# The last two attention steps of an audio tower: the softmax product on GpSimd, with sums and reciprocals in SBUF

## What is computed

```python
tokens = einsum('bnpd,edp->bne', patches(x), W) + b      # 16-sample patches, stride 8: 93 tokens
h = tokens
h = h + attn(layernorm(h))     # 8 heads of 64, a 3-tap causal convolution on q, k, v, ALiBi bias
h = h + ffn(layernorm(h))      # top-2 of 16 experts; each expert's hidden units are averaged over its tokens
# inside attn, per sequence and head (93 x 93 scores):
sim  = q @ k.T + bias, masked above the diagonal
attn = softmax(sim)            # exp(sim - max), divided by its row sum
out  = attn @ v
```

## Time and profile before

| | before |
|---|---|
| median of 3 runs | 741.98 us (741.1 to 743.17) |
| the profiled execution | 745.71 us, span 744.0 us, mean granted clock 0.984 |
| TensorE busy | 698.2 us, 94% |
| ScalarE busy | 603.1 us, 81% |
| VectorE busy | 572.5 us, 77% |
| GpSimd busy | 379.3 us, 51% |
| line 1242, product on VectorE | 64 instructions, 8 of them in steps 17 and 18 |

### The profile page before, as it was taken

How to read it: one execution, slowest core, us unless ns; L and a number is a source line. 1 busy time by engine, 2 the same in 40 slices (tenths; PEclk the granted TensorE clock), 3 DMA queues, 4 the chain that set the end, 5 groups by cost and what they waited for, 6 DMA issues and landing times.

```text
span 744.0 us, 21223 instructions
## 1 busy us (share of the span) xinstructions
PE 698.2 (94%) x6576; PEld 625.4 (84%) x6576; DVE 572.5 (77%) x1593; ACT 603.1 (81%) x2014; POOL 379.3 (51%) x392
## 2 busy tenths in 40 slices
PE   6889999999999999999999999998888898999996
PEld 6878888988888988889898989886776687999994
DVE  6166778788788788887787888788898768988876
ACT  4457889999898989899998989787877786899860
POOL 5652335676665665766666666554363557222200
PEclk9899999999999999999999999999999999999997
DMA  8132133341222211212212122102024123222206
GB/s 315 32 85 63 42 100 104 104 125 49 70 54 60 65 52 52 57 49 55 52 52 76 51 57 57 51 12 72 22 75 172 49 58 74 61 66 63 63 19 166
DMA packets 44274, 54.01 MB, mean 73 GB/s; under 512 B 13651, under 2 KB 31251, under 8 KB 43696
## 3 DMA queue, kind: packets, MB, share of 16 engines
q1 hardware_dynamic: 30048, 38.84, 17.9%
q0 software_dynamic: 12544, 12.87, 6.5%
q10 hardware_dynamic: 1616, 1.48, 0.6%
HBM read 42.69 MB, written 10.26 MB: 71 GB/s over the span
## 4 chain that ended last, share of the span: by engine, by line
PE 44%; DVE 28%; ACT 18%; issue 7%; DVEq 1%; DMA 1%; POOL 0%; ACTq 0%
ACT prob L909 11%; PE psTP L506 6%; DVE qkv L1101 5%; DVE qkv L1104 5%; PE psTP L508 5%; PE psTP L507 5%; PE psSO L788 4%; PE psTP L788 4%; DVE prob L1242 4%; PE psTP L580 3%; PE psSO L600 3%; PE psSO L655 3%; DVE rmin L1193 3%; PE psSO L636 3%; ACT qkv L878 3%
## 5 line engine op out<-in xcount | busy, mean ns | idle before, releaser
L1499 POOL DMA_INDIRECT expert_rows<-hn,slot x128 | 168.3, 1315 | 52.3 <-issue 32.0
L909 ACT ACTIVATE prob<-psSO,rmin 93x93 f32<-93x93 f32 x512 | 152.1, 355 | 9.1 <-DVE rmin L1193 8.6
L1417 POOL TENSOR_TENSOR x_lo<-x_raw,x_hi 128x752 fp32r<-128x752 f32 x58 | 105.0, 1811 | 46.4 <-ACT x_hi L870 45.9
L1101 DVE SCALAR_TENSOR_TENSOR qkv<-psTP,taps,qkv 128x368 f32<-128x368 f32 x192 | 112.7, 587 | 20.1 <-ACT qkv L878 18.4
L878 ACT ACTIVATE qkv<-psTP,taps 128x372 f32<-128x372 f32 x192 | 113.2, 590 | 9.2 <-PE psTP L508 8.7
L1104 DVE SCALAR_TENSOR_TENSOR qkv<-psTP,taps,qkv 128x364 f32<-128x364 f32 x192 | 114.5, 596 | 6.8
L909 ACT ACTIVATION_READ_ACCUMULATOR prob<-psSO,rmin 93x1 f32 x512 | 98.3, 192 | 0.0
L506 PE MATMUL psTP<-x_hi,wtok_hi 128*128 128x376 f32 x232 | 88.5, 381 | 1.0 <-POOL x_lo L1417 1.0
L506 PE MATMUL psTP<-xnT_hi,wqkv_hi 128*128 128x372 f32 x192 | 77.4, 403 | 8.3 <-DVE qkv L1104 7.7
L508 PE MATMUL psTP<-x_hi,wtok_lo 128*128 128x376 f32 x232 | 78.0, 336 | 0.0
L507 PE MATMUL psTP<-x_lo,wtok_hi 128*128 128x376 f32 x232 | 77.9, 336 | 0.0
(11 more groups left out here) (212 smaller groups left out, 1746.2 us busy)
## 6 DMA issues: line engine op xcount, KB each, us to landing
x_raw<-in_x SPq DMA_DIRECT2D x58, 376.0 KB
w1s<-in_w POOLq DMA_DIRECT2D x8, 512.0 KB
w<-in_w SPq DMA_DIRECT2D x4, 1024.0 KB
out<-resid SPq DMA_DIRECT2D x16, 160.0 KB, 2.6
xsE<-expert_rows SPq DMA_DIRECT2D x36, 64.0 KB, 2.0
xs<-expert_rows SPq DMA_DIRECT2D x36, 64.0 KB, 1.8
xs<-expert_rows POOLq DMA_DIRECT2D x36, 64.0 KB, 2.1
x_first_raw<-in_x SPq DMA_DIRECT2D x6, 376.0 KB, 6.6
```

The lines of the kernel that those rows point to most:

```text
L909: i = nc.scalar.activation(prob[:, a, hh, :], psS[:NT, a, hh * NT:(hh + 1) * NT], ACT.Exp, bias=rmin[:, a, hh:hh + 1], scale=-1.0, accum_o ...
L1101: nc.vector.scalar_tensor_tensor(dst[:, :, 1:NT], src[:, :, 0:NT - 1], taps[:, k, 1:2], dst[:, :, 1:NT], ALU.mult, ALU.add).then_inc(tap1_ ...
L1417: nc.gpsimd.tensor_tensor(lo[:, 0:PIECE], src, hi[:, 0:PIECE].bitcast(F32), ALU.subtract)\
L1499: nc.gpsimd.indirect_dma_start(rows, bass.IndirectOffsetOnAxis(slot[1 - u][:, c:c + 1], 0), hn[1 - u][:, c % GB, :], None)\
```

## The change

In steps 17 and 18 the sums and their reciprocals lie in two new SBUF tensors, `den_late` and `rden_late`, in place of PSUM, which GpSimd can then read. The reciprocal stays on VectorE. The product leaves VectorE's queue and becomes an instruction on GpSimd's, with the same tensor and a broadcast of the reciprocals. In GpSimd's slot it stands behind the four normalisation instructions (slot 1) and ahead of the slot's scatters. The other steps are as before.

```diff
--- before.py
+++ after.py
@@ -123,6 +123,7 @@
         wtok_raw = early0[:, 0:P * D].rearrange("p (s j e) -> p s j e", s=GB, j=4)
         wqkv_raw = early0[:, P * D:P * D + NBLK * 128].rearrange("p (k c) -> p k c", c=128)
         rmin = sb("rmin", [NT, 2, 4])
+        den_late, rden_late = sb("den_late", [NT, 2, 4]), sb("rden_late", [NT, 2, 4])
         prob = sb("prob", [NT, 2, 4, NT])
         probT = sb("probT", [NT, 2, 4, NT])
         attnT = sb("attnT", [128, QB, NT])
@@ -213,8 +214,7 @@
 
             if not isinstance(t, int) or t <= NG:
                 return psS[:NT, :, 4 * NT:4 * NT + 4], psS[:NT, :, 4 * NT + 4:4 * NT + 8]
-            bank = psTok if t == NG + 1 else psP[0]
-            return tuple(bank[:NT, at:at + 8].rearrange("p (a h) -> p a h", a=2) for at in (496, 504))
+            return den_late[:, :, :], rden_late[:, :, :]
 
         psOut = [psX4[:NT, :, :] for psX4 in psMix]
 
@@ -420,6 +420,10 @@
         def at(t, s, *slots):
 
             return isinstance(t, int) and (t - NG, s) in slots
+
+        def pool_divides(t):
+
+            return isinstance(t, int) and t > NG
 
         def late_slot(t, s):
 
@@ -1238,10 +1242,11 @@
                     if prev and f.proj and not f.tok and not f.norm:
                         residual(n, psWout)
                     if f.attn:
-                        dve.wait_ge(rden_done, n + 1)
-                        nc.vector.tensor_tensor(prob[:, :, :, :], prob[:, :, :, :],
-                                                rden.unsqueeze(3).broadcast_to([NT, 2, 4, NT]),
-                                                ALU.mult).then_inc(prob_ready, 1)
+                        if not pool_divides(t):
+                            dve.wait_ge(rden_done, n + 1)
+                            nc.vector.tensor_tensor(prob[:, :, :, :], prob[:, :, :, :],
+                                                    rden.unsqueeze(3).broadcast_to([NT, 2, 4, NT]),
+                                                    ALU.mult).then_inc(prob_ready, 1)
                     if f.proj and (f.tok or f.norm):
                         conv(t, u, 3 * s + 1)
                     if prev and (f.tok or f.norm or not f.proj) and not at(t, s, (2, 1), (2, 2), (2, 3)):
@@ -1481,6 +1486,13 @@
                         wait(pool, ln2_rstd, t - 3)
                         wait(pool, ln2_nmean, t - 3)
                         nc.gpsimd.tensor_tensor(shift2[:, :], nmean2[:, :], rstd2[:, :], ALU.mult).then_inc(ln2_shift, 1)
+                    if f.attn and pool_divides(t):
+                        n = (t - 3) * GB + s
+                        pool.wait_ge(exp_done, n * 2 + 2)
+                        pool.wait_ge(rden_done, n + 1)
+                        nc.gpsimd.tensor_tensor(prob[:, :, :, :], prob[:, :, :, :],
+                                                rden_late[:, :, :].unsqueeze(3).broadcast_to([NT, 2, 4, NT]),
+                                                ALU.mult).then_inc(prob_ready, 1)
                     if f.scat and f.attn:
                         scatter(t - 5, u, 2 * s, 2)
                     if f.scat and f.gate and not f.attn and s == 1:
```

## The result

The changed kernel takes 743.60 us (median of 20 runs, 741.86 to 747.86) for 742.19 of the kernel before (740.41 to 743.39) on the same chips: a ratio of 1.0024, with a 95% interval of 1.0013 to 1.0035, so 1.8 us slower (the two medians by themselves are 1.41 us apart). Run again later it came to 1.0036 (1.0016 to 1.0055), 2.7 us. It is slower, by less than 0.3% in the first comparison and a little more in the second. The forecast was 1.9 us slower.

The account below looks back on a forecast made before the run. Step 17 was taken as bound by VectorE's path and an equally long exponentials-product-transpose loop, step 18 by that loop. Step 17's -0.1 us and step 18's +2.0 make +1.9 on the 741.98 median: 743.9 us, range 741.0 to 747.8.

Parts of the forecast that it names:

- The pass on GpSimd: GpSimd's product over 93x744 takes 1.79 us, scaled from two-input passes over 752 columns; bounds 0.80 and 2.26.
- Hand-overs: Handing over to GpSimd and on to TensorE costs 0.07 and 0.05 us, in a reciprocal-to-TensorE path of 2.11 us.
- The sums in SBUF: ScalarE's 64 accumulator instructions writing to SBUF cost 0 us more each; bounds 0.03 less and 0.05 more.
- Rival D: Sums in SBUF are slower, 0.4 us on each of seven slots: +2.8 over the sum, 746.7 us; chance 0.14.
- The sign that was set for D: Accumulator rows longer than 0.19 us on average would show that slower sums in SBUF count.
- Step 17: Longer product loop makes slot 3's transposes 0.75 us late, but ScalarE's waits for VectorE's minimum shrink: net -0.1 us.
- Rival A: VectorE bounds step 17: 3.4 us saved there, step 18 costs 2.0, result 1.4 us faster, 740.6 us; chance 0.12.
- Slot 0: Step 18: loop from reciprocal to next exponentials grows from 2.98 to 3.19 us, +0.2.
- Slot 1: Step 18: product waits behind GpSimd's scatters and norm instructions, so transposes delay the exponentials: +0.8 us.
- the scatters, which the prediction blamed: Slot 0's two scatters in step 18, 1.29 us each, end later and push slot 1's norm instructions and product.
- Slot 2: Step 18: loop grows from 2.55 to 3.19 us, +0.65; later transposes add +0.15 before slot 3's reciprocal.
- Slot 3: Step 18: product ends about 0.2 us after TensorE finishes the work ahead of its transposes: +0.2 us.

Follow-up runs that it names:

- the sums in PSUM: Changed kernel with GpSimd still doing the product, but the exponentials' sums kept in PSUM and only the reciprocals in SBUF: ratio 0.9998.
- the product cut in two: Kernel before, with step 17's product split: GpSimd multiplies heads a = 1, VectorE heads a = 0; step 18 as before: ratio 0.9998.
- fillers: Small TensorE matmuls of zeros into an unused PSUM bank in step 18: ratio 0.9998 off the kernel before, 1.0006 off the changed kernel.
- the scatters later: Changed kernel with the two scatters of slot 0 of step 18 moved behind slot 1's product: ratio 1.0041.

## Why the prediction was right, and where it wasn't

**The direction and the size.** 1.8 us slower measured, 1.9 forecast, 1.46 to 1.9 in the stretch of the traces. The path was right: a longer loop over the product in step 18, and a relief of VectorE that is worth nothing. That the number came so near is partly luck, for two of the terms were mis-sized, against each other.

**The pass on GpSimd.** 1.79 us taken, 1.42 measured; within its bounds of 0.80 and 2.26, and nearer the middle than the row it was put at. Hand-overs were estimated at 0.12 us and took 0.20: the product starts 0.34 us after the start of a reciprocal of 0.20, TensorE 0.06 after the product's end. From the reciprocal to TensorE it is 1.83 and not 2.11. Why a pass with a broadcast operand and fewer partitions beats the scaled one was not tried.

**The sums in SBUF.** Taken at 0, measured 0.04 us for each exponential, inside the bounds of -0.03 and +0.05. The step that failed is the reason given for 0, that the exponential's row is longer than its accumulator's: what counts is when the next exponential starts. Rival D had the size of it, 0.4 us a slot for 0.31, but counted it on seven slots in full. Alone the new place brought 0.65 us in step 17 and 0.14 in step 18, because the loop waits elsewhere in 18.1 (copies of line 418, then the minimum) and 18.2 (slot 3's reciprocal hangs on the choice of experts). In the steady steps it does count in full. The sign that was set for D, accumulator rows over 0.19 us on average, decides nothing: in steps 17 and 18 they average 0.20 us before and 0.21 in the changed kernel. The Trainium skill (ScalarE: Activation LUTs, Step-by-step: what each stage is for) had the sign right: it calls PSUM the faster destination of an activation, and here, where the accumulator's output moved, it is 0.27 for 0.31 us.

**Step 17.** The shape was right, and the number by luck. Transposes 0.75 us late in slot 3 were forecast from the pass alone; they start 24.69 us after the first reciprocal for 23.91, 0.78. But with the sums in PSUM they start only 0.42 late (24.33), so nearly half is the sums, which were put at 0. ScalarE's waits for the minimum absorb it, from 1.24 and 0.82 us to 0.50 and nothing: +0.17 is left, for -0.1, or +0.66 where slot 17.3 is the longer one. Rival A, that VectorE bounds step 17, falls: the chain named VectorE, but ScalarE's queue was as long, VectorE stands idle 2.6 us more in a step that is no shorter, and with the product cut in two the trace is 0.3 to 0.5 us shorter and not 0.8 to 1.6.

**Step 18.** Slot 0: +0.24 for +0.2, but by another cause: the shorter pass left the loop where it was (5.39 with the sums in PSUM), and the sums made it 5.63. Slot 1: +0.50 for +0.8. The product starts 0.7 us late behind GpSimd's norm instructions; of that the scatters, which the prediction blamed, are 0.29, and the rest is the norm instructions' own time, which their order can't save, as the experiment with the product ahead shows. But the loss doesn't arrive by the transposes, as was forecast. They start 2.50 us after the reciprocal for 1.30, and yet the exponentials start only 3.98 after it for 3.71, since they wait for the minimum last in both kernels. The minimum is late behind the copy that the product held up; without the last 0.34 us of that wait they would have started 3.64 after the reciprocal, by these rows no later than before. The other 0.23 is the exponentials' wider spacing. The prediction had these copies end early beside GpSimd at no cost: wrong. Slot 2, from its reciprocal to that of slot 3: +0.54 for 0.65 + 0.15, as the transposes start 1.83 us after the reciprocal for 1.30. Slot 3: 0.01 for 0.2; the product, at 1.42 us, was done while TensorE was still at the work ahead of its transposes.

**What was not foreseen.** The traces give 1.46 or 1.9 us, by the length of slot 17.3, and the ratios stand for 1.8 and 2.7. The first needs no more than that slot; part of the second may be the granted clock. From slot 17.3 to the table load it fell in 5 of the 7 profiled executions of kernels with GpSimd's product in step 18 (not in the changed kernel's first one nor in the one with fillers), and once each with the sums in SBUF in both steps or in all and no product on GpSimd. It didn't fall there in either profile of the kernel before, in the one with fillers, nor with GpSimd in step 17 alone, with the whole product or half of it; the first profile of before and the one with fillers have a fall of their own some 12 us behind the table load. With the fillers the ratio is 0.0018 and 0.0030 lower than in the two comparisons without, 1.3 and 2.2 us, with intervals that meet at their ends. The times say the same and no more. The record gives each execution's mean granted clock. The changed kernel's four at 0.990 took 741.86 to 742.35 us, the three of the kernel before at 0.990 or above, in other comparisons, 740.76 to 741.18: some 1.1 us. Its six executions at 0.981 or lower took 743.91 to 747.86. But in the second comparison the three at 0.988 took 744.23 to 744.70, for 740.62 to 742.33 in the eight of before at 0.988, so there 2.4 us are lost at an equal mean clock (which can still hold a fall of 3 us, as that kernel's profile shows). So that the clock carries a part of the loss is supported; how much is open.

## What to carry to other kernels

An engine that the chain names as the bound can give nothing when relieved, as VectorE here, if a second engine's queue is as long: look for who waits for whom, and replay both loops. When a result changes its memory, look at the distance between the starts of the instructions that write it, not at their rows; 0.04 us on 512 small instructions was 18 us. And where a GpSimd pass over SBUF had started first, VectorE's copy from SBUF to SBUF ended only behind it, in slot 1 of step 18 of all seven traces that have both, so ask which copies stand ahead of something urgent.

## What the hardware showed

- An accumulator written to SBUF puts the next exponential 0.31 us after the last, one written to PSUM 0.27; the accumulator rows' own mean durations differ by only 0.01 us (0.21 and 0.20).
- A copy of 128x512 that started 0.08 us behind a GpSimd product took 1.63 us for 0.43, ending 0.29 after the product. With the scatters later, where the product was 0.38 us ahead of the copy, it took 1.33; with the sums in PSUM and 0.31 ahead 1.40; with the product ahead of the norm instructions and 0.74 ahead 0.97. In all seven traces with GpSimd's product in that slot the copy ended 0.28 or 0.29 us after the product.
- A two-input pass of GpSimd over 93x744 with a broadcast operand takes 1.42 us; without one, over 128x752, 1.80.
- The granted clock fell from 1.00 to 0.50 (2.4 to 1.2 GHz) for 3 to 17 us in or behind step 18, after stretches such as 5.90 of 8.20 or 3.96 of 6.00 us of TensorE's work. After 3.72 of 5.60 us in the changed kernel's first profile it stayed up, as it did after 3.71 of 5.39 in the second of the kernel before. It fell in some executions of a kernel and not in others, and the times of a kernel that has such stretches spread upward: above 744.5 us were 14 of 32 of the changed kernel and 6 of 43 of the kernel before beside it.
